# Queries and keys: split as token rows and turned by transposing transfers

## The chip, the cores and the metric

The program runs on one core of one Trainium2 chip. Its time is the device time in microseconds of one execution. Three executions of the kernel before took 1791.48, 1805.04 and 1810.17 us, median 1805.04. The core has five engines that run their own instruction streams in order: TensorE (PE, matrix products, with its weight loads as PEld), VectorE (DVE), ScalarE (ACT), GpSimd (POOL) and SyncE (SP), which here issues every transfer.

## The reference, cut to what matters

Sixteen images go through a template correlation (31x31 window, normalised by local mean and deviation), which gives 256 token rows of 256 features per image. Then, for each image:

```python
x = rmsnorm(h) * norm_w
q = (x @ Wq)  -> 16 heads of 64          k, v = x @ Wkv -> 8 heads of 64
q = q / |q| * (q_gamma + 1) * 8          k = k / |k| * (k_gamma + 1) * 8
sim = tanh(q @ k.T / 50) * 50 / 8        # 2 query heads share one key head
attn = softmax(causal(sim));  out = sum over heads(attn @ v) @ Wout
h = layernorm(h + out)
```

A five-matrix ternary network with gates and gelu and a second layer norm follow. The changed part is what lies between `x @ W` and `q @ k.T`: the length of each head's vector, the division by it, the gammas, the cut of each f32 value into a high and a low f16 part, and the turn from token rows (token on the partition) to feature rows (feature on the partition), which the product of queries and keys needs on both sides.

## The kernel before, in words

There are three stages: tokens (to 537 us of the profiled execution), attention (to about 1112 us) and the network (the rest). The change is in attention and in the last plane of the token stage, where the first image's attention inputs are made. Images go in groups of four, four groups; a group has 32 "heads" (8 per image, each a pair of query heads with one or two key heads).

Every engine runs the same list of named steps, each doing its own part, with semaphores between them. The list of a group comes from `attention_order` (L735): each step has a place on a scale on which head n's `score` stands at n, and the steps are sorted by it. The tables `IMAGE_AT`, `EDGE_AT` (first image of the next group) and `GROUP_AT` hold the places of the steps that make an image's inputs, counted from that image's first head. Since each engine keeps the order of its list, a step that waits holds up whatever stands behind it on its engine.

The steps, for one image and its two token blocks tb of 128 tokens:

- `make` (j = 4 tb + r): PE multiplies tokens by a 512-column piece of the weights (six matmuls); r = 0, 1 are queries, 2 keys, 3 values. ACT copies the result to `raw` (128 x 1536 f32 per block), or to `v` for r = 3.
- `square` and `sum`: ACT squares `raw` into `squares`, DVE sums each head's 64.
- `root`: DVE gets 1/length by three Newton rounds, eleven small instructions; one root per block.
- `scale`: DVE multiplies `raw` by it.
- `turn` (j = 4 tb + r, r = 0 to 2): PE transposes four 128x128 f32 pieces of `raw` into a bank of PSUM (`job`, four banks in a ring that all steps of the kind `make`, `turn`, `turn_h`, `turn_o`, `project` share). ACT writes the high f16 part, times gamma, to `q_hi` (four instructions of 128x128) or `k_hi` (one of 128x512).
- `low`: DVE subtracts that from the bank and writes `q_lo` or `k_lo`.
- `score` (n): PE, twelve short f16 matmuls into `sim`, which exists once; so head n's score waits for ACT's tanh of head n-1 (L1131). ACT then does tanh (L955) and exp (L958), POOL the causal mask (L888).
- `mix` (n), placed 2.5 places after its score: PE multiplies by `v`, DVE divides by the row sums (three short instructions, two for even heads).
- `turn_o`: PE transposes an image's output `o`, ACT copies it; `project`: PE multiplies by `Wout`, DVE adds it to h. The four `project` steps stand at the end of a group.

The `bits` steps read the network's weights piece by piece on DVE; SP loads each piece (`words`, L1198) and waits for the DVE step before.

Of the kernel before, what the change touches and what calls it, by code (L numbers as in the profile page):

```python
# [7 lines left out]
F16 = mybir.dt.float16  # L8
I32 = mybir.dt.int32
# [36 lines left out]
ROOTS = 1  # L46
# [5 lines left out]
BAND = RI * PR * TCOLS  # L52


class Shared:


    def __init__(self, nc, ctx):
# [31 lines left out]
        self.dump = sb("dump", [P, PR, D])  # L90
# [7 lines left out]
        self.o = sb("o", [P, 2, 2, HEADS, DH])  # L98
        sb("x_third_end", [P, plane - 4 * HEADS * DH])
# [12 lines left out]
        sb("xp_end", [P, XW - 4 * HEADS * (DH + 1)])  # L112
        self.job = ctx.enter_context(nc.psum_tensor("job", [P, BANKS, 512], F32))
# [50 lines left out]
def token_stage(nc, sh, at, X, XT, TF, TPAD, H, WORDS, WEIGHTS, WQKV, NW, GQ, GK):  # L164
# [6 lines left out]
    with ExitStack() as ctx:  # L171
# [11 lines left out]
        xt = sb("xt", [P, 2, XT_W])  # L183
# [48 lines left out]

        s_wlo_pool = sem("s_wlo_pool")
# [27 lines left out]
        def _(sp):  # L261
# [31 lines left out]
            def body(g, c, n, last):  # L293
# [53 lines left out]
        def _(act):  # L347
# [70 lines left out]
            def body(g, c, n, last):  # L418
# [14 lines left out]
                if more:  # L433
                    regroup(n + 1, 0)
                    regroup(n + 1, 1)
                    turned(n + 1, 0)
                else:
                    act.wait_ge(at.s_ones, 1)
                    at.scalar_steps(act, FIRST, 0, FIRST_PARTS["makes"])
                    act.wait_ge(sh.s_gamma, 10)  # L440
                    at.scalar_steps(act, FIRST, 0, FIRST_PARTS["turns"][0] + FIRST_PARTS["turns"][1])
# [10 lines left out]
        def _(dve):  # L452
# [6 lines left out]
            dve.sem_inc(at.s_ss, 1)  # L459

# [101 lines left out]
            def fold_span():  # L562
# [6 lines left out]
                dve.tensor_scalar(sh.gamma[:], sh.gamma[:], sh.span[:, 3:4], 1.0 / KEY_SCALE, ALU.mult, ALU.mult)\  # L569
                   .then_inc(sh.s_gamma, 1)  # L570
                dve.tensor_scalar(sh.span[:, 2:3], sh.span[:, 2:3], 1.0 / CLAMP, None, ALU.mult).then_inc(sh.s_gamma, 1)
                dve.wait_ge(sh.s_gamma, 10)

# [13 lines left out]
            def body(g, c, n, last):  # L587
# [21 lines left out]
                else:  # L609
                    at.vector_steps(dve, FIRST, 0, FIRST_PARTS["makes"])  # L610
                    scale(g, c, n, 0)
                    at.vector_steps(dve, FIRST, 0, FIRST_PARTS["turns"][0])
                    scale(g, c, n, 1)
                    at.vector_steps(dve, FIRST, 0, FIRST_PARTS["turns"][1])
# [6 lines left out]
        def _(pe):  # L621
# [19 lines left out]
            def correlate(c, n, b, start=0.0, end=1.0):  # L641
# [8 lines left out]
                size = len(terms)  # L650
                for t in range(int(start * size), int(end * size)):
                    x, i, xs, ws = terms[t]
# [6 lines left out]
                                    stop=(t == size - 1), skip_group_check=True)  # L659
                if end == 1.0:  # L660
                    ins.then_inc(s_conv, 1)
# [4 lines left out]
            def body(g, c, n, last):  # L666
                more = not (last and c == 2)
                if not more:
# [32 lines left out]
    ("make", 0): -8, ("make", 1): -8, ("make", 2): -7.725, ("square", 0): -7.18, ("make", 6): -6.997,  # L701
    ("sum", 0): -6.79, ("root", 0): -6.361, ("make", 4): -6.348, ("scale", 0): -6.321, ("make", 5): -5.839,
    ("make", 3): -5.512, ("square", 1): -5.39, ("sum", 1): -5.219, ("turn", 0): -4.545, ("make", 7): -4.423,
    ("root", 1): -4.413, ("low", 0): -4.389, ("turn", 1): -3.147, ("scale", 1): -2.767, ("low", 1): -2.619,
    ("turn", 2): -2.538, ("low", 2): -1.89, ("turn", 4): -1.49, ("low", 4): -1.23, ("turn", 5): -1.205,
    ("turn", 6): -1.068, ("low", 5): -1.063, ("low", 6): -0.99,
}
EDGE_AT = {
    ("make", 0): -8, ("make", 1): -8, ("make", 2): -8, ("square", 0): -7.718, ("make", 6): -6.743,
    ("sum", 0): -6.311, ("make", 4): -5.808, ("root", 0): -5.602, ("scale", 0): -5.343, ("make", 5): -4.841,  # L710
    ("square", 1): -4.533, ("make", 3): -3.75, ("sum", 1): -3.523, ("root", 1): -2.958, ("make", 7): -2.776,
    ("scale", 1): -1.653, ("turn", 0): -0.263, ("low", 0): 0.74, ("turn", 1): 1.01, ("turn", 2): 2.113,
    ("low", 1): 2.862, ("low", 2): 3.052, ("turn", 4): 3.86, ("low", 4): 4.18, ("turn", 5): 4.291,
    ("turn", 6): 4.697, ("low", 5): 4.751, ("low", 6): 4.828,
}
GROUP_AT = {
    ("rms_sum", 0): 4, ("rms_sum", 1): 6, ("rms_sum", 2): 8.635, ("rms_sum", 3): 15.072, ("turn_h", 0): 19.823,
    ("turn_h", 1): 19.97, ("turn_h", 2): 20.742, ("turn_h", 3): 21.416, ("project", 0): 36.821,
    ("project", 1): 37.209, ("project", 2): 37.906, ("project", 3): 38,
}  # L720
GROUP_AT.update({("rms_root", 0): 15.489, ("rms_scale", 0): 16.649, ("norm", 0): 38.109})
MIX_AT, TURN_O_AT, BITS_AT = LAG + 0.502, (1.332, 2.286), (2.334, 7.379)


def first_parts():

    tokens = [("turn_h", k) for k in range(4)]
    makes = [("make", 0, j) for j in (0, 1, 2)] + [("square", 0, 0), ("sum", 0, 0), ("root", 0, 0)]
    makes += [("make", 0, j) for j in (4, 5, 6)] + [("square", 0, 1), ("scale", 0, 0), ("sum", 0, 1), ("root", 0, 1)]
    makes += [("make", 0, j) for j in (3, 7)] + [("scale", 0, 1)]  # L730
    turns = [[(kind, 0, 4 * tb + r) for r in range(3) for kind in ("turn", "low")] for tb in range(2)]
    return {"tokens": tokens, "makes": makes, "turns": turns}
# [19 lines left out]
CHUNKS = 8  # L752
WORD_COLS = 2 * (D // P) * HID + 2 * (HID // P) * HID + (HID // P) * D
CW = WORD_COLS // (GROUPS * CHUNKS)


def emptied_on(step):

    if step[0] == "turn":
        return "queries" if step[2] % 4 < 2 else "keys"  # L760
# [3 lines left out]
class Stretch:  # L764


    def __init__(self, order, before, ahead):
        self.order, self.before, self.ahead = order, before, ahead
        self.jobs, self.counts = {}, []
        self.total = dict.fromkeys(("act", "dve", "queries", "keys"), 0)  # L770
        for step in order:
            job = ("turn",) + step[1:] if step[0] == "low" else step
            if step[0] in ("turn_h", "make", "turn", "turn_o", "project"):
                self.jobs[step] = len(self.jobs)
                self.counts.append(None)
                if step[0] == "turn":
                    continue
            elif step[0] != "low":
                continue
            on = emptied_on(job)  # L780
            self.total[on] += 1
            self.counts[self.jobs[job]] = (on, self.total[on])
# [10 lines left out]
FIRST = Stretch(FIRST_PARTS["tokens"] + FIRST_PARTS["makes"] + FIRST_PARTS["turns"][0] + FIRST_PARTS["turns"][1], False, 0)  # L793
# [11 lines left out]
class Attention:  # L805


    def __init__(self, nc, sh, ctx):
# [5 lines left out]
        self.rn, self.guess, self.slope = sh.rn, sh.guess, sh.slope  # L814
# [878 lines left out]
```

## Time and profile before

| | |
|---|---|
| median of three runs | 1805.04 us |
| profiled execution | 1788.73 us |
| its span on the core | 1786.9 us |
| mean granted TensorE clock | 0.994 of full speed |
| PE, DVE, ACT, POOL busy | 97, 64, 52, 24% |

The profiled execution is 0.9% under the median. A matmul's duration runs from its start to its modelled end, and the next one starts before that end; what a step costs on PE is therefore read from the distance between the starts of two steps, not from durations.

### The profile page before, as it was taken

The numbers are of one execution on the slowest core, as the hardware profiler recorded it, in microseconds if no ns is written. First come the engines' busy times: TensorE is split into PE (matmuls) and PEld (weight loads), VectorE is DVE, ScalarE is ACT, GpSimd is POOL, SyncE is SP. The second block draws the span as 40 slices with busy tenths as digits, with TensorE's granted clock in tenths as the row PEclk, the third lists the DMA queues.
The fourth block names the chain that finished last, engine by engine and source line by source line (L and its number), as shares of the span: only waits on it lengthen the run. The fifth ranks groups of instructions, "written<-read, shape, count | busy, mean of one in ns | idle before, by whom it ended". The sixth has DMA issues, their size and how long they took to land. (4 is left out here: it accounts for less than half of the span.)

```text
span 1786.9 us, 33009 instructions
## 1 busy us (share of the span) xinstructions
PE 1726.3 (97%) x12152; PEld 1509.7 (84%) x12152; DVE 1137.2 (64%) x2191; ACT 930.3 (52%) x1309; POOL 427.8 (24%) x515
## 2 busy tenths in 40 slices
PE   5999999999999999999999998999999999999998
PEld 5999998999987887888888887788888888888886
DVE  7899898898996877786877884423324141515242
ACT  8655555566658985895995994222222222222221
POOL 2000000000112222221222321434344333434343
PEclk9999999999999999999999999999999999999999
DMA  6322222223103002001100203600000000000000
GB/s 195 111 89 85 113 79 111 86 78 143 48 1 108 26 18 89 26 26 71 36 26 9 81 18 112 214 1 24 25 1 24 1 25 1 24 1 24 1 13 13
DMA packets 26421, 97.23 MB, mean 54 GB/s; under 512 B 3081, under 2 KB 11401, under 8 KB 21010
## 3 DMA queue, kind: packets, MB, share of 16 engines
q1 hardware_dynamic: 26258, 94.96, 15.5%
q8 instruction: 115, 1.88, 0.4%
q14 instruction: 48, 0.39, 0.1%
HBM read 82.33 MB, written 24.15 MB: 60 GB/s over the span
## 5 line engine op out<-in xcount | busy, mean ns | idle before, releaser
L658 PE MATMUL conv<-w,x 128*128 128x368 f16 (+5 forms) x3960 | 452.7, 277 | 3.8 <-issue 3.8
L658 PEld LDWEIGHTS conv<-w,x 128*128 128x128 f16 x3960 | 427.2, 146 | 27.9 <-issue 4.5
L1439 ACT ACTIVATE raw_c<-ring,sh 128x512 f32<-128x512 f32 x128 | 87.6, 689 | 334.3 <-PE ring L1542 334.2
L1451 DVE CAST ha_hi<-raw_c 128x512 fp32r<-128x512 f32 x128 | 85.2, 665 | 201.0 <-ACT raw_c L1439 198.8
L888 POOL TENSOR_SCALAR_AFFINE_SELECT probs<-probs 128x256 f32<-128x256 f32 x256 | 129.9, 530 | 342.2 <-ACT probs L958 342.2
L1398 POOL TENSOR_TENSOR ha_lo<-raw_c,ha_hi 128x512 fp32r<-128x512 f32 x128 | 165.3, 1291 | 189.5 <-DVE ha_hi L1451 189.5
L1542 PE MATMUL ring<-ha_hi,wh 128*128 128x512 f32 x512 | 199.4, 389 | 0.9 <-POOL ha_lo L1398 0.9
L1542 PE MATMUL ring<-ha_lo,wh 128*128 128x512 f32 x512 | 199.2, 389 | 0.0
L1542 PE MATMUL ring<-hb_lo,wh 128*128 128x512 f32 x512 | 199.2, 389 | 0.0
L1542 PE MATMUL ring<-hb_hi,wh 128*128 128x512 f32 x512 | 199.2, 389 | 0.0
L1151 PEld LDWEIGHTS mixed<-v,probs 128*128 128x128 f32 x1536 | 185.5, 193 | 10.7 <-POOL probs L888 1.7
L1151 PE MATMUL mixed<-v,probs 128*128 128x65 f32 x1536 | 192.2, 275 | 1.9 <-DVE o L1044 1.8
L1451 DVE CAST hb_hi<-raw_c 128x512 fp32r<-128x512 f32 x64 | 35.7, 558 | 187.3 <-ACT raw_c L1439 187.0
L379 ACT ACTIVATE lines<-job 128x512 f32<-128x512 f32 x96 | 50.0, 605 | 167.8 <-PE job L638 167.7
L955 ACT ACTIVATE probs<-sim,span 128x768 f32<-128x768 f32 x128 | 115.8, 905 | 12.6 <-PE sim L1136 12.0
L472 DVE TENSOR_TENSOR_SCAN box<-lines 128x271 f32<-128x271 f32 x192 | 120.2, 699 | 3.5 <-ACT lines L379 3.5
L1114 PE MATMUL job<-wqkv_hi,ht_hi 128*128 128x512 f32 x256 | 110.5, 432 | 7.6 <-PEq L171 3.6
L1398 POOL TENSOR_TENSOR hb_lo<-raw_c,hb_hi 128x512 fp32r<-128x512 f32 x64 | 82.5, 1290 | 140.5 <-DVE hb_hi L1451 140.5
L1542 PEld LDWEIGHTS ring<-ha_hi,wh 128*128 128x128 f32 x512 | 96.1, 188 | 21.6 <-POOL ha_lo L1398 1.6
L1542 PEld LDWEIGHTS ring<-hb_lo,wh 128*128 128x128 f32 x512 | 96.1, 188 | 20.0
L1542 PEld LDWEIGHTS ring<-ha_lo,wh 128*128 128x128 f32 x512 | 96.1, 188 | 19.9
L1542 PEld LDWEIGHTS ring<-hb_hi,wh 128*128 128x128 f32 x512 | 96.1, 188 | 19.9
(161 smaller groups left out, 3198.5 us busy)
## 6 DMA issues: line engine op xcount, KB each, us to landing
xt<-x_columns_in SPq DMA_DIRECT2D x12, 1163.0 KB, 5.2
xp<-x_patches_in SPq DMA_DIRECT2D x12, 1152.0 KB, 5.1
hidden_words<-hidden_weights_in SPq DMA_DIRECT2D x8, 1408.0 KB, 8.5
words<-hidden_words SPq DMA_DIRECT2D x32, 352.0 KB, 3.0
wh<-hidden_words SPq DMA_DIRECT2D x8, 1024.0 KB, 10.0
tokens<-planes SPq DMA_DIRECT2D x4, 1024.0 KB, 4.6
h<-tokens SPq DMA_DIRECT2D x4, 1024.0 KB, 7.3
attended<-h SPq DMA_DIRECT2D x8, 512.0 KB, 3.5
```

The costliest lines, as they stand in the source:

```text
L379: act.activation(dst, turn[:, k % 4], ACT.Copy).then_inc(s_across, 1)
L472: return dve.tensor_tensor_scan(out, line[:, TH:TH + SCAN], line[:, 0:SCAN], 0.0, ALU.add, ALU.subtract)
L658: ins = pe.matmul(out, xs[:, c, RI - 1 - i:RI - 1 - i + NR, :, x].rearrange("p r g -> p (r g)"), w, start=(t == 0), stop=(t == size - 1), ...
L888: ins = pool.affine_select(out=diag, in_=diag, compare_op=ALU.is_ge, fill=0.0, base=0, pattern=[[0, 2], [1, P]], channel_multiplier=-1)
L955: act.activation(self.probs[:, n % 4], self.sim[:, :, 0:3 * P], ACT.Tanh, scale=self.span[:, 2:3]).then_inc(self.s_tanh, 1)
L1114: ins = pe.matmul(bank, x[:, f, img % GI, P * tb:P * tb + P], w[:, f, 512 * r:512 * r + 512], start=(t == 0), stop=(t == len(terms) - 1))
L1151: ins = pe.matmul(out, self.probs[:, n % 4, m, at:at + P], self.v[:, img % 2, jb, 2 * (hd // 2) + m], start=(jb == 0), stop=(jb == ib), sk ...
L1398: pool.tensor_tensor(dst[1][:, u % KH], raw[:, u % 4], dst[0][:, u % KH].bitcast(F32), ALU.subtract).then_inc(s_lo, 1)
L1439: act.activation(raw[:, u % 4], bank, ACT.Gelu, scale=scale[:, m:m + 1]).then_inc(s_gelu, 1)
L1451: dve.tensor_copy(dst[0][:, u % KH], raw[:, u % 4]).then_inc(s_hi, 1)
L1542: ins = pe.matmul(bank, a, b, start=start, stop=False, skip_group_check=True)
```

## The change

High and low parts are now cut out of `raw` while the rows are still tokens, and four transfers that transpose on their way bring them to `q_hi`, `k_hi`, `q_lo`, `k_lo`. In detail:

- The gammas are held as rows (`gain`, 128 x 1024, two new inputs of 512 KB each, loaded at the end of the token stage); DVE folds them there. One `root` serves both token blocks of an image and ends with a small multiply by `KEY_SCALE`. `scale` gets a second DVE instruction, queries times `gain`.
- `turn` is gone. `high` is one ACT copy of 128 x 1536 to `hi_tok` (f16); `low` one DVE subtraction of 128 x 1536 to `lo_tok` (f16). Each buffer exists once: `high` waits until the transfers out of `hi_tok` have landed and until the `low` before it is done; `low` waits for `high` and for the transfers out of `lo_tok`.
- SP gets `sync_steps`: after each `high` and each `low` two transfers, 128 x 1024 (queries) and 128 x 512 (keys), f16, from SBUF to SBUF with transpose. The first head's `score` of an image waits for all eight transfers of the image.
- The tables have new places; first image, later images and the next group's first image now have the same ones. `turn_o` stands directly behind the `mix` of an image's last head. Some buffers move, and `dump` has two rows for eight.

```diff
 IMAGE_AT = {
-    ("make", 0): -8, ("make", 1): -8, ("make", 2): -7.725, ("square", 0): -7.18, ("make", 6): -6.997,
...
+    ("make", 0): -7.9, ("make", 1): -7.5, ("make", 2): -7.1, ("square", 0): -6.9, ("make", 4): -6.5,
+    ("make", 5): -6.0, ("sum", 0): -6.0, ("make", 6): -5.5, ("square", 1): -5.3, ("sum", 1): -4.8, ("root", 0): -4.2,
+    ("make", 3): -4.0, ("scale", 0): -3.8, ("make", 7): -3.5, ("high", 0): -3.2, ("low", 0): -2.9,
+    ("scale", 1): -2.6, ("high", 1): -2.0, ("low", 1): -1.7,
...
-MIX_AT, TURN_O_AT, BITS_AT = LAG + 0.502, (1.332, 2.286), (2.334, 7.379)
+MIX_AT, TURN_O_AT, BITS_AT = LAG + 0.5, (0.5, 0.51), (2.48, 6.48)
...
+    def sync_steps(self, sp, run, g, steps, between=None):
...
+                if kind == "high":
+                    sp.wait_ge(self.s_high, t + 1)
+                    sp.wait_ge(self.s_score, self.image(g, img) * HEADS + 8)
+                    settle(sp, self.s_settle)
+                    sp.dma_start(self.q_hi[:, img % 2, :, cols], self.hi_tok[:, 0:HEADS * P], transpose=True).then_inc(self.s_flip_hi, 16)
+                    sp.dma_start(self.k_hi[:, img % 2, :, cols], self.hi_tok[:, HEADS * P:QK], transpose=True).then_inc(self.s_flip_hi, 16)
...
-            elif kind == "turn":
...
-                        ins = act.activation(self.q_hi[:, img % 2, u, cols], bank[:, e * P:(e + 1) * P], ACT.Copy,
-                                             scale=self.gamma[:, u:u + 1])
...
+            elif kind == "high":
+                t = self.image(g, step[1]) * 2 + step[2]
+                act.wait_ge(self.s_qn, t + 1)
+                act.wait_ge(self.s_low, t + 2)
+                if run is not FIRST or step[2]:
+                    act.wait_ge(self.s_flip_hi, 32 * t)
+                act.activation(self.hi_tok[:], self.raw[:, step[2]], ACT.Copy).then_inc(self.s_high, 1)
...
-                dve.tensor_tensor(heads, heads, by, ALU.mult).then_inc(self.s_qn, 1)
+                dve.tensor_tensor(heads, heads, by, ALU.mult).then_inc(self.s_scaled, 1)
+                dve.wait_ge(self.s_scaled, t + 1)
+                queries = self.raw[:, tb, 0:HEADS * P]
+                dve.tensor_tensor(queries, queries, self.gain, ALU.mult).then_inc(self.s_qn, 1)
...
+                dve.wait_ge(self.s_high, t + 1)
+                if run is not FIRST or step[2]:
+                    dve.wait_ge(self.s_flip_lo, 32 * t)
+                dve.tensor_tensor(self.lo_tok[:], self.raw[:, step[2]], self.hi_tok[:], ALU.subtract).then_inc(self.s_low, 1)
...
-            elif kind == "turn":
-                img, tb, r = step[1], step[2] // 4, step[2] % 4
-                bank = free_bank(run, g, step)
-                pe.wait_ge(self.s_qn, self.image(g, img) * 2 + tb + 1)
-                for e in range(4):
-                    c = (4 * r + e) * P
-                    ins = pe.transpose(bank[:, e * P:(e + 1) * P], self.raw[:, tb, c:c + P], self.ident[:])
-                ins.then_inc(self.s_job, 1)
...
-                    pe.wait_ge(self.s_emptied["queries"], self.image(g, img) * 4 + 4)
-                    pe.wait_ge(self.s_emptied["keys"], self.image(g, img) * 2 + 2)
+                    pe.wait_ge(self.s_flip_hi, 64 * self.image(g, img) + 64)
+                    pe.wait_ge(self.s_flip_lo, 64 * self.image(g, img) + 64)
...
+                dve.wait_ge(s_rows, 32)
+                dve.tensor_scalar(sh.gain, sh.gain, 1.0, sh.span[:, 3:4], ALU.add, ALU.mult).then_inc(sh.s_gamma, 1)
...
-                    at.tensor_steps(pe, FIRST, 0, FIRST_PARTS["turns"][0])
-                    correlate(c, n, 3, 0.0, 0.5)
-                    at.tensor_steps(pe, FIRST, 0, FIRST_PARTS["turns"][1])
-                    correlate(c, n, 3, 0.5, 1.0)
+                    correlate(c, n, 3)
```

What the tables do is seen in ACT's list. In the changed kernel, for one image inside a group, from the tanh and exp of the fifth head before the image to those of the second before it (`v<-job` are the `make` steps of the values, `hi_tok<-raw` the two `high`):

```order
L980 ACTIVATE probs<-sim,span 128x768 [waits b_mix,b_score]
L983 ACTIVATE probs<-probs 128x768 [waits b_tanh]
...
L960 ACTIVATE v<-job 128x8x64 [waits b_mix,b_job]
L974 REGISTER_ALU [waits b_low,b_qn]
L975 ACTIVATE hi_tok<-raw 128x1536 [waits b_flip_hi]
...
L980 ACTIVATE probs<-sim,span 128x768 [waits b_mix,b_score]
L983 ACTIVATE probs<-probs 128x768 [waits b_tanh]
L972 REGISTER_ALU [waits b_qn]
L974 REGISTER_ALU [waits b_low]
L975 ACTIVATE hi_tok<-raw 128x1536 [waits b_flip_hi]
```

Two copies of 1536 columns, each with a wait for `b_qn` (the DVE `scale`), now stand between the tanh and exp of neighbouring heads. Before, the same engine had short pieces there, whose waits are for PE's `turn` (in brackets what an instruction waits for):

```order
L945 ACTIVATE q_hi<-job,gamma 128x128 [waits b_score,b_job]
L945 ACTIVATE q_hi<-job,gamma 128x128 x3
...
L955 ACTIVATE probs<-sim,span 128x768 [waits b_mix,b_score]
L958 ACTIVATE probs<-probs 128x768 [waits b_tanh]
L916 ACTIVATE ht_hi<-job 128x4x32x4 [waits b_job]
L949 ACTIVATE k_hi<-job 128x4x128 [waits b_score,b_job]
```

On DVE the changed list around the two `scale` steps of an image is (`raw<-raw,rn` and `raw<-raw,lines` are `scale`, `lo_tok` is `low`, `rl`, `o` and `parts` are `mix`):

```order
L1046 TENSOR_TENSOR raw<-raw,rn 128x1536
L1049 TENSOR_TENSOR raw<-raw,lines 128x1024
...
L1061 RECIPROCAL rl<-mixed 128x4
L1065 TENSOR_TENSOR o<-mixed,rl 128x2x128
...
L1055 TENSOR_TENSOR lo_tok<-raw,hi_tok 128x1536
L1046 TENSOR_TENSOR raw<-raw,rn 128x1536
L1049 TENSOR_TENSOR raw<-raw,lines 128x1024
```

The first `low` stands between the two `scale` steps and waits for ACT's first `high`; before, both roots and both scales had `turn` pieces between them.

## Rows read from the trace of the kernel before

**Rows 1.** The page, busy time of each engine over the span:
```profile
PE 1726.3 (97%) x12152; PEld 1509.7 (84%) x12152; DVE 1137.2 (64%) x2191; ACT 930.3 (52%) x1309; POOL 427.8 (24%) x515
```

**Rows 2.** Waits of PE, 560 to 1060 us: total, times, longest:
```profile
PE mixed L1151 <- DVE o L1044: 1.8, 2, 1.4
```

**Rows 3.** Busy time by windows, attention: start:end, length, busy (count), clock, DMA, GB/s:
```profile
1000.00:1060.00 60.00, 60.00 (x517) 51.16 (x517) 46.44 (x123) 53.45 (x87) 15.53 (x30) 1.00 0.09 26
```

**Rows 4.** Timeline of PE, attention: start, duration, instruction:
```profile
696.14 1.45 PE L1151 MATMUL mixed<-v,probs 128*128 128x65 f32 x12
697.52 0.28 PE L1136 MATMUL sim<-q_hi,k_hi 64*128 64x256 f16 x2
...
698.12 0.66 PE L1123 MATMUL job<-ident,raw 128*128 128x128 f32 x4
698.62 1.45 PE L1151 MATMUL mixed<-v,probs 128*128 128x65 f32 x12
699.88 0.48 PE L1114 MATMUL job<-wqkv_hi,ht_hi 128*128 128x512 f32 x1
...
701.45 0.28 PE L1136 MATMUL sim<-q_hi,k_hi 64*128 64x256 f16 x2
```

**Rows 5.** Groups by line and shape, 560 to 1060 us: count, busy, mean ns, idle before:
```profile
L955 ACT ACTIVATE probs<-sim,span 128x768 f32<-128x768 f32 x112 | 101.4, 905 | 10.0 <-PE sim L1136 9.5
L958 ACT ACTIVATE probs<-probs 128x768 f32<-128x768 f32 x111 | 93.8, 845 | 3.5
L1018 DVE TENSOR_TENSOR raw<-raw,rn 128x1536 f32<-128x1536 f32 x28 | 49.8, 1778 | 0.4
L990 DVE TENSOR_REDUCE rn<-lines 128x24 f32<-128x1536 f32 x28 | 49.0, 1749 | 7.7 <-ACT lines L936 7.5
L924 ACT ACTIVATE raw<-job 128x512 f32<-128x512 f32 x84 | 49.0, 587 | 66.8 <-PE job L1114 66.7
L936 ACT ACTIVATE lines<-raw 128x1536 f32<-128x1536 f32 x28 | 41.5, 1480 | 0.7
L1048 DVE TENSOR_TENSOR o<-o,parts 128x256 f32<-128x256 f32 x56 | 24.8, 443 | 1.9
L1044 DVE TENSOR_TENSOR parts<-mixed,rl 128x256 f32<-128x256 f32 x56 | 23.8, 424 | 1.9
```

**Rows 6.** Timeline of DVE, one root, first and last of eleven instructions:
```profile
646.19 0.38 DVE L996 TENSOR_SCALAR rn<-rn 128x24 f32<-128x24 f32 x1
...
648.56 0.18 DVE L1011 SCALAR_TENSOR_TENSOR rn<-slope_b,guess_b 128x24 f32<-128x24 f32 x1
```

**Rows 7.** DMA issues of the page and the view: KB each, us to landing:
```profile
w<-padded_template SPq DMA_DIRECT2D x6, 636.0 KB, 9.3
out<-y SPq DMA_DIRECT2D x16, 256.0 KB, 2.5
xt<-w_qkv_in SPq DMA_DIRECT2D x1, 1024.0 KB, 7.0
```

**Rows 8.** Timeline of PE, the `project` steps that end a group:
```profile
1099.64 10.31 PE L1172 MATMUL job<-w_out,ot 128*128 128x256 f32 x47
```

**Rows 9.** Timeline of PE around its longest wait in attention:
```profile
708.51 2.79 PE L1151 MATMUL mixed<-v,probs 128*128 128x65 f32 x12 [1.35 <-DVE o L1044]
711.10 2.76 PE L1123 MATMUL job<-ident,raw 128*128 128x128 f32 x12
```

**Rows 10.** Busy time by windows of 5 us, columns as in rows 3:
```profile
710.00:715.00 5.00, 5.00 (x32) 4.29 (x31) 4.75 (x18) 2.94 (x11) 0.77 (x2) 0.50 0.02 3
1090.00:1095.00 5.00, 2.91 (x23) 2.43 (x22) 3.01 (x8) 1.14 (x2) 0.30 (x1) 1.00 0.00 0
```

**Rows 11.** Timeline of DVE and PE, last plane of the token stage:
```profile
481.71 5.01 DVE L472 TENSOR_TENSOR_SCAN box<-lines 128x271 f32<-128x271 f32 x8
...
490.22 0.15 DVE L564 TENSOR_SCALAR span<-span 128x1 f32<-128x1 f32 x1
...
522.44 1.49 PE L1123 MATMUL job<-ident,raw 128*128 128x128 f32 x12
```

More of the change, by code:

```diff
@@ L45 @@
 QK = QH * DH + HEADS * DH
-ROOTS = 1
+ROOTS = 2
 BANKS = 4
@@ L300, in body @@
                     sp.dma_start(WORDS[rows], WEIGHTS[rows]).then_inc(s_copies, 16)
+                if last and c == 2:
+                    sp.wait_ge(s_box, 2 * LAST + 4)
+                    for dst, src in ((sh.gain, GQ_ROWS), (sh.gain_k, GK_ROWS)):
+                        sp.dma_start(dst, src).then_inc(s_rows, 16)
+                    at.sync_steps(sp, FIRST, 0, FIRST_PARTS["flips"])
                 if c == 2:
@@ L649, in correlate @@
                 quarter = 4 * PC * b
-                size = len(terms)
-                for t in range(int(start * size), int(end * size)):
-                    x, i, xs, ws = terms[t]
+                for t, (x, i, xs, ws) in enumerate(terms):
                     first = PC * (x - 1)
@@ L700 @@
 IMAGE_AT = {
-    ("make", 0): -8, ("make", 1): -8, ("make", 2): -7.725, ("square", 0): -7.18, ("make", 6): -6.997,
[L702 to L705, printed above, removed]
@@ L710 @@
[L710 to L714, printed above, removed]
+    ("make", 0): -7.9, ("make", 1): -7.5, ("make", 2): -7.1, ("square", 0): -6.9, ("make", 4): -6.5,
@@ L715 @@
+    ("make", 5): -6.0, ("sum", 0): -6.0, ("make", 6): -5.5, ("square", 1): -5.3, ("sum", 1): -4.8, ("root", 0): -4.2,
+    ("make", 3): -4.0, ("scale", 0): -3.8, ("make", 7): -3.5, ("high", 0): -3.2, ("low", 0): -2.9,
+    ("scale", 1): -2.6, ("high", 1): -2.0, ("low", 1): -1.7,
 }
 GROUP_AT = {
-    ("rms_sum", 0): 4, ("rms_sum", 1): 6, ("rms_sum", 2): 8.635, ("rms_sum", 3): 15.072, ("turn_h", 0): 19.823,
-    ("turn_h", 1): 19.97, ("turn_h", 2): 20.742, ("turn_h", 3): 21.416, ("project", 0): 36.821,
@@ L725, in first_parts @@
+GROUP_AT.update({("rms_root", 0): 18.4, ("rms_scale", 0): 20.4, ("norm", 0): 39})
+MIX_AT, TURN_O_AT, BITS_AT = LAG + 0.5, (0.5, 0.51), (2.48, 6.48)
 def first_parts():
     tokens = [("turn_h", k) for k in range(4)]
-    makes = [("make", 0, j) for j in (0, 1, 2)] + [("square", 0, 0), ("sum", 0, 0), ("root", 0, 0)]
-    makes += [("make", 0, j) for j in (4, 5, 6)] + [("square", 0, 1), ("scale", 0, 0), ("sum", 0, 1), ("root", 0, 1)]
-    makes += [("make", 0, j) for j in (3, 7)] + [("scale", 0, 1)]
@@ L731, in first_parts @@
-    turns = [[(kind, 0, 4 * tb + r) for r in range(3) for kind in ("turn", "low")] for tb in range(2)]
-    return {"tokens": tokens, "makes": makes, "turns": turns}
+    makes = [("make", 0, j) for j in (0, 1, 2)] + [("square", 0, 0), ("sum", 0, 0)]
+    makes += [("make", 0, j) for j in (4, 5, 6)] + [("square", 0, 1), ("sum", 0, 1), ("root", 0, 0)]
+    makes += [("make", 0, j) for j in (3, 7)]
+    flips = [("scale", 0, 0), ("high", 0, 0), ("scale", 0, 1), ("low", 0, 0), ("high", 0, 1), ("low", 0, 1)]
```

191 lines of the change are left out of this document (102 added, 89 removed).

## The prediction

> **What bounds the kernel now.** I read the page first: PE is busy 97% of the span, every other engine far less [rows 1]. So a step taken off PE is worth its full length wherever PE never waits. Whether it waits in attention is told by the waits of PE from 560 to 1060 us: six kinds, 8.7 us in all of 500, the longest single one 1.35 us for DVE's `mix` [rows 2, 9]. The windows then say how near the others are: in a full stretch of 60 us ACT is busy 53.5 and DVE 46.4 [rows 3]. PE is the bound, ACT is six us behind it, and the present order lets ACT and DVE work in short pieces under PE's cover.
>
> The costs on PE come from distances between starts [rows 4]: `mix` 1.4 us (696.14 to 697.52), `score` 0.6 (697.52 to 698.12), four transposes of a `turn` 0.50 (698.12 to 698.62), one `make` 1.45 to 1.57 (699.88 to 701.45). The four `project` steps of a group are 32 matmuls with two records each; at 10.31 us for 47 records [rows 8] the 64 are 14 us.
>
> **Removed from PE.** 90 `turn` steps in the attention stage (six for each of 15 images) at 0.50 us: 45 us; the first image's six are two lots of 12 transposes of about 1.3 us in the token stage [rows 11]: 2.7 us. Together **-47.7 us**, all of it on the path as long as PE stays the bound.
>
> **Moved and added on ACT and DVE.** Both engines get less work: ACT loses the q_hi and k_hi pieces and gets two copies of 1536 columns; DVE loses one of two roots. Busy time is not what matters, though: the new order makes one long chain between two points of PE's own list. I walk it for one image inside a group. M is the moment when PE ends `make` 6, the last that fills `raw`; all times are us after M. Durations are the means of [rows 5] unless said.
>
> - ACT ends an exp, copies the bank (0.59) and squares (1.48): 2.7. DVE sums (1.75): 4.4; a `mix` (0.44 + 0.42 + about 0.18 for the small one): 5.5; the root, eleven instructions in 2.55 us [rows 6]: 8.1. `scale` is 1.78, and the multiply by `gain` by the same rate 1024/1536 of that, 1.19: 11.1.
> - ACT, which keeps its order, has waited for that with `high`. A copy of 1536 columns is nearest to the square of the same size, 1.48: 12.6. Only now comes the tanh (0.9) of the head behind it: 13.5.
> - PE has between M and there four `mix`, three `score` less one, two `make`: 4 x 1.4 + 2 x 0.6 + 2 x 1.45, and the score whose tanh is late, 0.6: 10.3. The next `score` needs the tanh at 13.5, since `sim` exists once. **PE waits 3.2 us.**
> - DVE does a `mix`, then `low` for block 0 (1.78, as the f32 `scale` of that size) from 12.6 to 14.4, then `scale` and `gain` of block 1 (3.0): 17.4. ACT's second `high` ends at 18.9, the next tanh at 19.8. PE, done with a `score` and a `mix` at 15.5, **waits 4.3 us**; it then has a `score` and a `mix`, until 21.8.
> - DVE's `low` of block 1 ends at 20.7. Then two transfers (393 KB) must land before the image's first `score`. With L for that pair, PE **waits L - 1.1 us**.
>
> **The price of the transfers, L.** No transposing transfer is in the trace. Queries' 262 KB are like the 256 KB of the output, which land in 2.5 us [rows 7]; that is the low bound. The transfer with the smallest pieces is w<-padded_template, 636 KB in 9.3 us [rows 7]; at its rate the pair takes 5.7 us. A transpose handles small pieces, so I go nearer to the second: L = 4.5. If the pair does not only take that long to land but occupies the path for it, four pairs of an image line up behind each other from 12.6 on: at 5.7 each the last lands at 12.6 + 22.8 = 35.4, and the last wait is 13.6 instead of 3.4. Another such price sits beside these: by the Trainium skill, "Advanced Engine Details and Errata", section "X-Bar Transpose (TRN2)", a transposing transfer runs about as fast as a plain one; the sum would then lie at the low bound of L, some 24 us under mine.
>
> **Counted.** Twelve images (the second to fourth of each group, and in the last group too) have all three waits: 12 x (3.2 + 4.3 + 3.4) = **+131 us**. The first images of groups 2 to 4 are made at the end of the group before; there the `project` steps, 14 us, lie between the last `low` and the first `score` and cover the transfers: 3 x 7.5 = **+22 us**. `turn_o` now stands directly behind the `mix` that it needs; DVE takes 1.04 us and the way there and back for it, while before a score and a make lay between: 1.3 us x 12 = **+16 us**. The waits of before are contained in the new ones: **-9 us**.
>
> **Token stage.** fold_span ran at 490.2 us [rows 11]. It now waits for 2 x 512 KB that are asked for when the box sums are done, 486.7 [rows 11]; one MB took 7.0 us to land [rows 7], so 3.5 us of waiting, and two multiplies of 1024 columns, 2.4. The weights' low parts, for which PE's first `make` waits, stand behind these on DVE and come later by that: **+6 us**. SP's queue costs nothing more: `words` loads have 5 to 10 us between request and use, and the stores at the end of a group come before the next group's first `high`.
>
> **Clock.** After the 1.35 us wait at 707 us PE's granted clock was 0.50 in the next window, the 1.2 GHz level, and `mix` took 2.6 us for 1.4 [rows 9, 10]; in the window 1090 to 1095, with PE idle 2.1 us, it stayed at 1.00 [rows 10]. So a wait may cost some 3 us more, or nothing. Slow work between two waits is hidden in them; behind the third wait it is not. I take 2.4 us for twelve: **+29 us** (both ends: 0, and 3.2 us also after each `turn_o`, 77).
>
> **Sum.** -47.7 + 131 + 22 + 16 - 9 + 6 + 29 = +147 on the profiled 1788.7: 1936. The median of the runs before lies 16 us above that execution; with nearly all of this added, the forecast is **1950 us**, 8% slower.
>
> **Rivals.**
>
> 1. *The chain has slack and only PE's saving is left.* For it speaks that ACT and DVE get less work and that the durations of `low` and `gain` are mine. It needs the chain of 20.7 us to be shorter by ten, since PE's own work beside it is 14 us. Then 1789 - 48 - 9 + 6: about 1740. Chance 8%. Half of that slack ends near the old time, within 1%: 4%.
> 2. *The transfers themselves are the bound.* If a pair occupies the path for twice the slow row's price, 11.4 us, the four pairs of an image end at 12.6 + 45.6 = 58.2, the last wait is 36 us instead of 3.4, and twelve of them make +390; the three covered images add about 50: 2380 us. It decides from about 8 us a pair, where they pass my range. Against it is that this is half the rate of the slowest large transfer in the rows, and no more than that. A rule of the Trainium skill would do this: "VectorE: DVE Perf Modes", section "The three transpose paths", gives 1309 ns for a 128x128 block by transfer, against 390 ns on TensorE. By it, an estimate, a pair of 12 blocks would take 15.7 us and the time would be about 2650. This trace puts the TensorE side at 0.125 us a block [rows 4], well under that page's figure, so I do not lean on its other one. Chance 12%.
> 3. *My forecast*, between 1835 and 2120: chance 76%.
>
> **Range.** Low end: L = 2.5 (-24), no clock loss (-29), half of the two ACT waits (-56): 1950 - 109, 1840. High end: pairs that line up at 5.7 us (+122) and the clock's upper bound (+48): 2120. With the small tails inside, 1835 to 2120 holds about 8 in 10. About 1% is what a measurement of this kernel can tell from none (its runs spread over 1%): faster 0.08, same 0.04, slower 0.88.
>
> **What would show it.** In the profile of the changed kernel: PE's waits in attention grow from 9 us per 500 to over 100, and name ACT's tanh (L980) and the transfers, for `sim`; ACT sits idle before `hi_tok` for DVE's `raw`, about 3 us each; `turn_o` waits for `o`; the landing of q_lo and k_lo gives L directly; the clock is under 0.99 in attention. Wrong would be: a chain that keeps ahead of PE, so that PE is still busy without waits; or landings above 8 us, which make SP's queue the chain.

## The result, and the profile after

The changed kernel takes 2000.48 us (median of four executions, 1992.07 to 2004.81) against 1805.07 us: a ratio of 1.1106, 95% interval 1.1047 to 1.1166. It is 11% slower; forecast were 1950 us and 8%. The profiled execution took 2004.05 us, its span is 2002.2 us, 215 us above that of before.

The page of the changed kernel; the second row is TensorE's granted clock in tenths, in 40 slices of the span. Its first row answers to [rows 1]:

```profile
PE 1801.3 (90%) x11768; PEld 1563.9 (78%) x11768; DVE 1129.5 (56%) x1809; ACT 897.4 (45%) x1053; POOL 444.7 (22%) x515
PEclk9999999999977868877788777579999999999999
DMA packets 129073, 122.99 MB, mean 61 GB/s; under 512 B 105513, under 2 KB 113833, under 8 KB 123698
```

PE has 384 fewer instructions and is busy 75 us *longer*. The clock row says where: only in the attention stage. The same stage by windows (start:end, length, busy of PE, PEld, DVE, ACT, POOL, clock, DMA share, GB/s), from the store of the tokens to the end of the last `project`, first before, then after:

```profile
537.00:1110.00 573.00, 558.11 (x4584) 475.69 (x4584) 426.16 (x1145) 451.77 (x768) 142.68 (x272) 0.99 0.15 49
```
```profile
538.00:1328.00 790.00, 634.56 (x4224) 531.49 (x4224) 415.29 (x785) 421.40 (x528) 159.00 (x272) 0.78 0.27 65
```

The stage has all of the change: 573 became 790, +217. ACT and DVE are busy less than before, as read from the diff. PE's idle time (length less busy) went from 15 to 155 us, **+140**; its busy time from 558 to 635, **+77**, though 45 us of transposes are gone from it. So, by subtraction, some 77 + 45 = **122 us** are time that matmuls took longer than before, at a mean clock of 0.78 for 0.99.

What PE waits for over the whole span (total, times, longest), where [rows 2] had DVE's `mix` alone on top:

```profile
PE sim L1149 <- ACT probs L980: 95.6, 30, 4.4
PE job L1173 <- DVE o L1069: 19.5, 16, 1.3
PE job L666 <- ACT down_m L391: 19.0, 2, 16.5
PE sim L1149 <- DMA k_lo<-lo_tok: 15.2, 8, 2.5
PE sim L1149 <- issue: 12.1, 5, 3.4
```

The third row is in the kernel before as well, outside attention. The first is the tanh behind a `high`, twice for each of 15 images. Three of the five `issue` waits, 1.9 us each, stand where an image's wait for `k_lo` stands, in the last group; so the third waits are 21.0 us in eleven images. The other two, 3.35 and 3.05 us, stand right behind `project`, when the transfers had long landed; what they are for isn't shown. ACT's own waits from 545 to 1320 us say why the tanh is late:

```profile
ACT hi_tok L975 <- DVE raw L1049: 109.2, 30, 4.5
```

**One image walked.** PE, DVE and ACT around the second image, each row with start, duration and in brackets the idle time before it and its releaser. `make` 6 ends at 597.18, which is M of the prediction.

```profile
597.18 1.45 PE L1164 MATMUL mixed<-v,probs 128*128 128x65 f32 x12
...
606.17 1.55 PE L1164 MATMUL mixed<-v,probs 128*128 128x65 f32 x12
611.03 0.40 PE L1149 MATMUL sim<-q_hi,k_hi 64*128 64x256 f16 x2 [3.31 <-ACT probs L980]
612.10 2.82 PE L1164 MATMUL mixed<-v,probs 128*128 128x65 f32 x12
617.59 0.39 PE L1149 MATMUL sim<-q_hi,k_hi 64*128 64x256 f16 x2 [2.67 <-ACT probs L980]
618.66 2.82 PE L1164 MATMUL mixed<-v,probs 128*128 128x65 f32 x12
624.01 0.40 PE L1149 MATMUL sim<-q_hi,k_hi 64*128 64x256 f16 x2 [2.53 <-DMA k_lo<-lo_tok]
```
```profile
607.36 1.22 DVE L1049 TENSOR_TENSOR raw<-raw,lines 128x1024 f32<-128x1024 f32 x1
610.31 1.76 DVE L1055 TENSOR_TENSOR lo_tok<-raw,hi_tok 128x1536 f16<-128x1536 f32 x1 [1.17 <-ACT hi_tok L975]
...
616.98 1.76 DVE L1055 TENSOR_TENSOR lo_tok<-raw,hi_tok 128x1536 f16<-128x1536 f32 x1 [0.89 <-DMA k_lo<-lo_tok]
```
```profile
608.70 1.48 ACT L975 ACTIVATE hi_tok<-raw 128x1536 f16<-128x1536 f32 x1 [3.64 <-DVE raw L1049]
610.09 0.88 ACT L980 ACTIVATE probs<-sim,span 128x768 f32<-128x768 f32 x1
```

`gain` ends at M + 11.4 (forecast 11.1), `high` at 13.0 (12.6), the late tanh at 13.8 (13.5), and PE waits 3.31 us (3.2). This is the chain that the prediction walked. PE stands 3.3 us, ACT has stood 3.6 before it, and DVE works without a pause up to the end of `gain`. What follows differs: the `mix` at 612.10 takes 2.82 us, twice its 1.45, so PE arrives at the second wait later and finds 2.67 us of it left (forecast 4.3).

The windows of the same 40 us show the clock itself, with columns as above:

```profile
600.00:605.00 5.00, 5.00 (x39) 4.05 (x39) 4.49 (x15) 3.92 (x6) 1.02 (x3) 1.00 0.02 5
605.00:610.00 5.00, 2.72 (x30) 2.38 (x29) 4.00 (x6) 1.36 (x2) 0.51 (x2) 0.89 0.00 0
610.00:615.00 5.00, 3.90 (x24) 3.33 (x24) 4.66 (x3) 1.81 (x3) 2.99 (x2) 0.50 0.56 107
615.00:620.00 5.00, 2.41 (x18) 2.02 (x19) 4.01 (x8) 4.70 (x8) 1.77 (x3) 0.50 0.67 127
620.00:625.00 5.00, 2.47 (x19) 2.00 (x19) 1.33 (x4) 2.55 (x9) 0.78 (x3) 0.50 0.81 155
625.00:630.00 5.00, 5.00 (x18) 3.91 (x14) 0.00 (x0) 2.34 (x3) 0.76 (x2) 0.56 0.01 4
630.00:635.00 5.00, 5.00 (x39) 4.05 (x38) 0.61 (x2) 3.48 (x8) 0.00 (x0) 1.00 0.00 0
```

Full (2.4 GHz) until the first wait, half (1.2 GHz) through all three waits, and full again only some 6 us after the last, while PE is in the `make` that follows: some 20 us at half speed for this image, of which PE works some 13. The last image of the last group has no `make` behind its first score, only `mix`, `score` and `turn_o`. There the clock stays at half from its first score, 1268 us, until PE is in `project`, 1314 us: 42 us of work, some 21 of them for the clock (an estimate, half of the work, from the two levels). One window out of it:

```profile
1282.00:1287.00 5.00, 5.00 (x33) 4.27 (x35) 0.87 (x4) 1.74 (x2) 1.53 (x4) 0.50 1.02 416
```

**The transfers.** SP's issues of the second block of that image, and the view's rows for all 128 (median us from issue to landing at the end), in the place of [rows 7]:

```profile
616.85 1.23 SPq L887 DMA_TRANSPOSE q_hi<-hi_tok  x1
618.12 1.28 SPq L888 DMA_TRANSPOSE k_hi<-hi_tok  x1
619.59 1.23 SPq L893 DMA_TRANSPOSE q_lo<-lo_tok  x1
620.87 1.29 SPq L894 DMA_TRANSPOSE k_lo<-lo_tok  x1
```
```profile
q_hi<-hi_tok SPq DMA_TRANSPOSE x32, 3.2
k_hi<-hi_tok SPq DMA_TRANSPOSE x32, 2.5
q_lo<-lo_tok SPq DMA_TRANSPOSE x32, 3.2
k_lo<-lo_tok SPq DMA_TRANSPOSE x32, 2.6
```

262 KB land in 3.2 us. But the issue instructions hold SP for 1.25 us each, one after the other. The last `low` ended at 618.74; SP, still issuing for `high`, began on q_lo at 619.59, and PE went on at 624.01: 5.3 us for the pair, of which 3.4 are SP's.

### The profile page after: what moved, and what is told of

It reads as the page before. It is cut to its first block and busy times, and to the rows that moved or that the text cites. A ratio compares the mean times of both kernels' runs of the same rounds, so it can differ in the third digit from the quotient of the medians.

```text
span 2002.2 us, 31467 instructions
## 1 busy us (share of the span) xinstructions
PE 1801.3 (90%) x11768; PEld 1563.9 (78%) x11768; DVE 1129.5 (56%) x1809; ACT 897.4 (45%) x1053; POOL 444.7 (22%) x515
## 2 busy tenths in 40 slices
DMA packets 129073, 122.99 MB, mean 61 GB/s; under 512 B 105513, under 2 KB 113833, under 8 KB 123698
## 5 line engine op out<-in xcount | busy, mean ns | idle before, releaser
L914 POOL TENSOR_SCALAR_AFFINE_SELECT probs<-probs 128x256 f32<-128x256 f32 x256 | 146.8, 597 | 518.9 <-ACT probs L983 518.9
L1164 PEld LDWEIGHTS mixed<-v,probs 128*128 128x128 f32 x1536 | 238.9, 239 | 14.4 <-issue 6.3
L1164 PE MATMUL mixed<-v,probs 128*128 128x65 f32 x1536 | 246.4, 324 | 0.0
L1474 DVE CAST ha_hi<-raw_c 128x512 fp32r<-128x512 f32 x128 | 90.6, 708 | 201.0 <-ACT raw_c L1462 198.8
L1149 PE MATMUL sim<-q_hi,k_hi 64*128 64x256 f16 (+1 forms) x512 | 73.9, 284 | 127.0 <-ACT probs L980 95.6
L1061 DVE RECIPROCAL rl<-mixed 128x4 f32<-128x4 f32 x128 | 22.7, 177 | 229.5 <-PE mixed L1164 229.5
L1149 PEld LDWEIGHTS sim<-q_hi,k_hi 64*128 64x128 f16 x512 | 27.9, 104 | 158.6 <-ACT probs L980 100.4
L1135 PE MATMUL job<-wqkv_hi,ht_hi 128*128 128x512 f32 x256 | 121.0, 473 | 10.1 <-DVE ht_lo L1010 9.8
```

The lines of the kernel that those rows point to most:

```text
L914: ins = pool.affine_select(out=diag, in_=diag, compare_op=ALU.is_ge, fill=0.0, base=0, pattern=[[0, 2], [1, P]], channel_multiplier=-1)
L1135: ins = pe.matmul(bank, x[:, f, img % GI, P * tb:P * tb + P], w[:, f, 512 * r:512 * r + 512], start=(t == 0), stop=(t == len(terms) - 1))
L1149: ins = pe.matmul(self.sim[:, m, 2 * P * jb:2 * P * jb + P * (2 - jb)], k[rows, img % 2, hd // 2, P * jb:P * jb + P], q[rows, img % 2, hd, ...
L1164: ins = pe.matmul(out, self.probs[:, n % 4, m, at:at + P], self.v[:, img % 2, jb, 2 * (hd // 2) + m], start=(jb == 0), stop=(jb == ib), sk ...
L1474: dve.tensor_copy(dst[0][:, u % KH], raw[:, u % 4]).then_inc(s_hi, 1)
```

## The experiments

All are of one core. Each is compared with runs of the kernel before on the same chip; the ratio is to them. Differences in us to the changed kernel (2000.48) are across chips, on which the medians of the kernel before lie up to 6 us apart; small ones mean little. For each stage the windows run between the same two points as above.

**Only the tables.** The changed kernel, its steps placed anew so that every link of an image's chain has work of PE beside it. Steps move by up to 3.6 places (entries set several to a line here); the tables of the next group's first image and of the group's own steps are fitted anew likewise and not shown:

```diff
 IMAGE_AT = {
-    ("make", 0): -7.9, ("make", 1): -7.5, ("make", 2): -7.1, ("square", 0): -6.9, ("make", 4): -6.5,
-    ("make", 5): -6.0, ("sum", 0): -6.0, ("make", 6): -5.5, ("square", 1): -5.3, ("sum", 1): -4.8, ("root", 0): -4.2,
-    ("make", 3): -4.0, ("scale", 0): -3.8, ("make", 7): -3.5, ("high", 0): -3.2, ("low", 0): -2.9,
-    ("scale", 1): -2.6, ("high", 1): -2.0, ("low", 1): -1.7,
+    ("make", 1): -11.13, ("make", 0): -9.99, ("make", 2): -9.85, ("square", 0): -9.16, ("sum", 0): -8.17,
+    ("make", 4): -8.15, ("make", 6): -7.87, ("make", 5): -7.67, ("square", 1): -7.38, ("sum", 1): -7.3,
+    ("root", 0): -6.33, ("scale", 0): -5.77, ("make", 3): -5.03, ("make", 7): -4.98, ("high", 0): -4.69,
+    ("low", 0): -4.45, ("scale", 1): -3.98, ("high", 1): -2.48, ("low", 1): -2.18,
...
-MIX_AT, TURN_O_AT, BITS_AT = LAG + 0.5, (0.5, 0.51), (2.48, 6.48)
+MIX_AT, TURN_O_AT, BITS_AT = LAG + 0.5, (1.79, 2.71), (0.31, 7.01)
```

> The changed kernel with other numbers in IMAGE_AT, EDGE_AT, GROUP_AT and TURN_O_AT and nothing else: every instruction is the same, only their order in each engine's list differs. The makes of an image begin some two to four places earlier, high and low stand where DVE and ACT have already finished what they wait for, turn_o 1 stands two places later. If the loss is the ACT-DVE chain against PE's list (my reading), the 127 us of waits for sim fall under 40 and most of the clock loss goes with them: 1760 to 1830 us. If the transfers or the work they need are the bound, the order is of no use: 1950 us or more.

Measured 1826.72 us, ratio 1.0128 (1.0062 to 1.0195): 174 us less than the changed kernel, by the order alone. From `make` 6 to `high` 0 there are now 3.2 places instead of 2.3, and from `scale` 1 to `high` 1 1.5 instead of 0.6. The waits of PE over the span, and the stage:

```profile
PE sim L1190 <- ACT probs L1021: 12.3, 9, 2.4
```
```profile
538.00:1148.00 610.00, 557.32 (x4224) 467.48 (x4224) 411.08 (x785) 418.93 (x528) 159.79 (x272) 0.91 0.36 84
```

95.6 us of waits for the tanh have become 12.3, and with them the clock rose from 0.78 to 0.91. The change itself is not what costs 11%; its tables are. Yet the median is still 16 us above that of before, and the profiled stage 37 us longer than before, not 45 shorter. One place shows part of why: before the last image's first score PE stands until 1089.60 (SP issued `k_lo` at 1086.08), and the rows after it are at half speed for 45 us (first window, last of them, and the one after):

```profile
1089.60 0.40 PE L1190 MATMUL sim<-q_hi,k_hi 64*128 64x256 f16 x2 [4.57 <-issue]
```
```profile
1090.00:1095.00 5.00, 5.00 (x38) 4.27 (x33) 1.50 (x3) 2.13 (x3) 0.76 (x2) 0.50 0.50 139
...
1130.00:1135.00 5.00, 3.78 (x10) 2.84 (x9) 0.00 (x0) 1.46 (x2) 0.13 (x1) 0.50 0.00 0
1135.00:1140.00 5.00, 5.00 (x23) 4.30 (x23) 1.44 (x3) 0.00 (x0) 0.00 (x0) 0.94 0.00 0
```

**The clock apart from the waits.** PE does idle transposes, which nothing reads, where it would stand: 24 and 32 ahead of the two late scores, 12 ahead of an image's first, 8 ahead of `turn_o`.

```diff
+                fill = {0: 12, 6: 24, 7: 32}.get(hd, 0) if n and (run is BODY or n < 25) else 0
+                if fill:
+                    ahead = next(s for s in run.order[run.order.index(step):] if s in run.jobs)
+                    spare = free_bank(run, g, ahead)
+                    for _ in range(fill):
+                        pe.transpose(spare[:, 0:P], self.ident[:], self.ident[:])
...
                 bank = free_bank(run, g, step)
+                for _ in range(0 if b else 8):
+                    pe.transpose(bank[:, 0:P], self.ident[:], self.ident[:])
```

> The changed kernel, with idle work on PE just before its predicted waits: 24, 32 and 12 transposes of the identity (0.11 us each at full clock, into a free bank of job) before the score of the seventh and eighth head of an image and of the first of the next, and 8 before the first turn_o. Nothing reads them. If the lower granted clock is what makes the loss larger than the waits alone, the granted clock in attention rises from 0.79 to over 0.92 and the time falls by 50 to 90 us, to 1910 to 1950. If the clock matters little, because slow work hides in the waits, the time stays at 2000 or grows.

Measured 1967.67 us, ratio 1.0896 (1.0830 to 1.0962), 33 us less than the changed kernel, less than expected. The stage:

```profile
538.00:1291.00 753.00, 673.43 (x5336) 582.06 (x5336) 415.19 (x785) 420.33 (x528) 163.74 (x272) 0.95 0.30 68
```

The clock did come back, 0.78 to 0.95; the waits for the tanh fell to 31.2 us. But the 1112 added transposes are themselves PE work, 0.125 us each by [rows 4], 139 us, and not all of it lies where PE would have stood. So this run shows that the clock comes back when PE's standing is filled, and that it leaves the stage 37 us shorter, the fill's own time paid; it isn't a clean measure of what the slow clock costs. **With about half of that fill**:

```diff
-                fill = {0: 12, 6: 24, 7: 32}.get(hd, 0) if n and (run is BODY or n < 25) else 0
+                fill = {0: 6, 6: 16, 7: 16}.get(hd, 0) if n and (run is BODY or n < 25) else 0
...
-                for _ in range(0 if b else 8):
+                for _ in range(0 if b else 5):
```

> As e2_warm, with 16, 16 and 6 idle transposes before the three scores and 5 before turn_o, where e2 had 24, 32, 12 and 8: 43 in all instead of 76 for each image, 3.6 us less of added work, 54 us over fifteen images. If e2 gained only 33 us because its added work was longer than the waits, less of it is better as long as the clock holds: 1935 to 1960. If the clock falls again with the shorter filling: 1970 to 2000.

Measured 1970.93 us, ratio 1.0929 (1.0851 to 1.1006): no gain over the full fill. The stage's clock is 0.89, the waits for the tanh 56.5 us. Less fill gave lower clock and longer waits in like measure. The second of the two expectations held.

**Is it the transposing?** The four kinds of transfer move the same bytes to the same tiles without transposing; the queries and keys are then not the right ones.

```diff
-                    sp.dma_start(self.q_hi[:, img % 2, :, cols], self.hi_tok[:, 0:HEADS * P], transpose=True).then_inc(self.s_flip_hi, 16)
+                    sp.dma_start(self.q_hi[:, img % 2, :, cols], self.hi_tok[:, 0:HEADS * P].rearrange("p (e t) -> p e t", t=P)).then_inc(self.s_flip_hi, 16)
```

> The changed kernel with its 128 transposing transfers made plain copies of the same bytes between the same buffers, so q_hi to k_lo hold token rows (attention is computed on untransposed data). By the chain theory the transfers only set the last of the three waits (15 us of waits for k_lo in all): 1980 to 2002 us. If transposing is what costs, through its landing, SP's issue time of 1.25 us each, or what it does to other engines: under 1930.

Measured 1997.80 us, ratio 1.1061 (1.0995 to 1.1127), 2.7 us under the changed kernel, within the latter's spread (1992.07 to 2004.81). The landings, and PE's waits:

```profile
q_hi<-hi_tok SPq DMA_DIRECT2D x32, 256.0 KB, 2.9
k_lo<-lo_tok SPq DMA_DIRECT2D x32, 128.0 KB, 3.0
```
```profile
PE sim L1149 <- ACT probs L980: 95.5, 30, 4.6
PE sim L1149 <- DMA k_lo<-lo_tok: 7.3, 6, 1.3
```

The waits for `k_lo` halve; SP issues a plain transfer in 0.6 to 0.7 us. The two ACT waits stay. So transposing is not the cost. A plain copy is a transfer too, so that transfers as such are no bound (rival 2) is shown by their landings and by the retimed kernel, which has the same 128 of them.

**Is it the chain?** The multiply by `gain`, 1.26 us, is left out of each `scale`; queries lack their gamma.

```diff
-                dve.tensor_tensor(heads, heads, by, ALU.mult).then_inc(self.s_scaled, 1)
-                dve.wait_ge(self.s_scaled, t + 1)
-                queries = self.raw[:, tb, 0:HEADS * P]
-                dve.tensor_tensor(queries, queries, self.gain, ALU.mult).then_inc(self.s_qn, 1)
+                dve.tensor_tensor(heads, heads, by, ALU.mult).then_inc(self.s_qn, 1)
```

> The changed kernel without the second instruction of scale (queries times gain, 128 x 1024 on DVE); the queries' gammas are left out. Chain theory: each image has two of them, 1.15 us each, on the path between make 6 and the last low, for 15 images 35 us, and a little clock: 1945 to 1975. If DVE is not on the path: 1995 to 2005.

Measured 1962.16 us, ratio 1.0852 (1.0785 to 1.0919): 38 us less (by the ratios, 46), for 32 x 1.26 = 40 us of DVE work, on an engine that is busy half of the stage. Waits for the tanh are 76.2 instead of 95.6; the stage is 41 us shorter, half of it idle time, half PE's busy time at a clock of 0.80 instead of 0.78. DVE is on the path, between PE's `make` 6 and ACT's `high`, as walked.

**`turn_o` in both directions.** In the kernel before it is put directly behind its `mix`; in the changed one it is put back to the places of before.

```diff
-MIX_AT, TURN_O_AT, BITS_AT = LAG + 0.502, (1.332, 2.286), (2.334, 7.379)
+MIX_AT, TURN_O_AT, BITS_AT = LAG + 0.502, (0.51, 0.52), (2.334, 7.379)
```
```diff
-MIX_AT, TURN_O_AT, BITS_AT = LAG + 0.5, (0.5, 0.51), (2.48, 6.48)
+MIX_AT, TURN_O_AT, BITS_AT = LAG + 0.5, (1.332, 2.286), (2.48, 6.48)
```

> The kernel before with one number pair of the change: turn_o directly behind the mix of an image's last head (TURN_O_AT 0.51, 0.52 for 1.332, 2.286). As predicted, PE waits 1.3 us for o at each of the sixteen: +10 to +25 us, more where the clock falls after it. If the wait is hidden otherwise: within 5 us of the kernel before.

Measured 1820.87 us, ratio 1.0128 (1.0066 to 1.0189), about 15 us against the 1806.21 of before; PE waits for `o` 23.1 us in 16, where before it was 4.5 in 5.

> The changed kernel with turn_o at the places of before (1.332, 2.286). If the 19.5 us of waits for o are lost time of their own, 1970 to 1990; if they only delay PE where it waits for ACT or DVE anyway, within 5 us of 2000.

Measured 1983.59 us, ratio 1.1009 (1.0953 to 1.1066), 17 us less than the changed kernel, and PE waits for `o` only 5.1 us. The term of +16 stands, from both sides: these waits are lost time of their own.

**What is PE's saving worth?** The kernel before, with one transpose of the four in each `turn`; three quarters of queries and keys aren't turned. PE loses 96 x 3 x 0.125 = 36 us of work (32 at the 0.11 us that the expectation takes).

```diff
-                for e in range(4):
+                for e in range(1):
```

> The kernel before with one of the four transposes of each turn step (the other three pieces of queries and keys are left out), to measure what the PE work that the change removes is worth by itself. By the forecast's price of 0.11 us each, 288 transposes are 32 us: 1770 to 1780 if PE is the bound throughout. If ACT or DVE, whose work stays, takes over: 1790 to 1806.

Measured 1805.02 us, ratio 1.0010 (0.9969 to 1.0050) in ten executions against thirteen: nothing. The stage:

```profile
537.00:1127.00 590.00, 565.89 (x4314) 473.93 (x4314) 424.09 (x1145) 447.51 (x768) 139.32 (x269) 0.93 0.14 47
```

In the stage PE has 270 transposes less, 34 us, yet it is busy 566 us, 8 more than in the profile of before, and idle 24 instead of 15. The granted clock is 0.93 for 0.99. The two profiles are not alike, though: that of before is one of its shorter executions. Among executions of 1807 to 1809 us those of before have a mean clock of 0.980 to 0.983 over the whole span, these 0.969 to 0.972. One hundredth of the clock is some 18 us of PE's work (an estimate, 1734 x 0.0105), so about half of the 36 us came back as slower work; the rest should be waits, but no profile of such an execution of before was taken. The time fell in the range expected if ACT or DVE takes over, which is only a part of it.

The longest stretch at half clock starts at the first score of the last image. PE, now earlier there, waits 2.40 us for DVE's `k_lo` (first row), where before it waited 1.19 (second). After it the clock is 0.50 until `project`, 45 us later; in the kernel before it stays at 1.00 through the same steps (a window of each):

```profile
1069.50 0.28 PE L1136 MATMUL sim<-q_hi,k_hi 64*128 64x256 f16 x2 [2.40 <-DVE k_lo L1032]
1070.57 0.28 PE L1136 MATMUL sim<-q_hi,k_hi 64*128 64x256 f16 x2 [1.19 <-DVE k_lo L1032]
```
```profile
1080.00:1100.00 20.00, 20.00 (x127) 17.53 (x126) 4.69 (x13) 9.76 (x12) 3.45 (x10) 0.50 0.49 179
1075.00:1095.00 20.00, 17.18 (x184) 15.48 (x178) 10.88 (x27) 13.44 (x17) 6.55 (x14) 1.00 0.50 184
```

That stretch holds 40 us of work, some 20 of them for the clock (estimated as above). The runs do not show what decides whether a wait is followed by half clock: in the kernel before, one of 1.35 us was [rows 9, 10].

**Both together.** The retimed kernel, with idle transposes at the places where it still stands:

```diff
+                warm(run, g, step, {2: 18, 24: 34 if run is FINAL else 6}.get(n, 0))
...
+                warm(run, g, step, 9 if (img, b) == (3, 0) else 0)
...
+                    warm(run, g, step, 9)
```

(`warm` is the loop of the fill above; another 16 stand ahead of a group's first `make` of the next.)

> e1_retimed with idle transposes of the identity at the waits that its profile still shows on PE: 18 before the score of a group's third head, 34 before the first score of the last image of the last group (6 in the others), 9 before that image's turn_o and before project, 16 before the next group's first make. If the 16 us that e1 lies above the kernel before are the clock (it was at 0.50 from 1090 to 1135 us), it is near 1.00 there and the time is 1775 to 1805, at or under the kernel before. If they are work or waits, it stays at 1820 to 1835.

Measured 1801.41 us in twelve executions, ratio 0.9990 (0.9960 to 1.0020): on a level with the kernel before, not better. The stage:

```profile
538.00:1129.00 591.00, 561.25 (x4468) 477.17 (x4468) 411.94 (x785) 417.97 (x528) 163.53 (x272) 0.96 0.37 87
```

244 added transposes, some 30 us of work by the same price, bring the clock from 0.91 to 0.96 and the stage from 610 to 591. In the last image, after 34 of them, the clock is back at full long before `project`:

```profile
1090.00:1095.00 5.00, 5.00 (x64) 4.38 (x62) 1.22 (x4) 3.54 (x5) 0.96 (x3) 1.00 0.88 307
```

No version beats the kernel before by what can be measured.

## Why the prediction was right, and where its sizes were off

- **Mechanism and direction: right.** The walk's times held within 0.4 us up to the first wait; leaving out `gain` and moving the steps alone confirm that the chain DVE, ACT, PE of one image against PE's own order is what costs. Rival 1 (slack) is refuted by the 30 waits, rival 2 by the landing of 3.2 us, where it needed 8 for a pair, and by the retimed kernel.
- **The waits: near, in part by luck.** Terms for new waits gave 131 + 22 + 16 - 9 = 160; PE's idle time grew by 140. The waits for the tanh are 95.6 where 15 x 7.5 = 112 were forecast; the second is shorter than walked because the slow `mix` ahead of it fills part of it, which the prediction said of slow work between waits but did not subtract. Waits that it lacked make up for some of this: 6.4 us in two scores behind `project`, which it took as covered; 6.8 us in three of an image's `make` for `ht_lo`; 4.7 us in four of `project` for `ot` (1.6 in one before). `turn_o` waits at all sixteen images, 19.5 us, not at twelve.
- **L: too small, and for another reason.** Walked with 4.5, measured 5.3 us at the second image. Its size isn't the landing (3.2 and 2.6) but SP, which each issue holds for 1.25 us. Still the third wait came out at 2.53 us there and 21.0 us in eleven images, not 12 x 3.4 = 41: at the second image PE reached it 2.5 us later than walked, again at half clock. By the Trainium skill, "Advanced Engine Details and Errata", section "X-Bar Transpose (TRN2)", transposing transfers run about as fast as plain ones; the landings agree (3.2 against 2.9 us for 262 KB). The Trainium skill, "VectorE: DVE Perf Modes", section "The three transpose paths", gives 1309 ns for a 128x128 block by transfer. As a price per block of a larger transfer, which is how the estimate of 15.7 us for a pair took it, this does not hold here: eight such blocks land in 3.2 us, not 10.5.
- **The clock: the term that failed.** It was +29 (2.4 us for each of twelve images, bounds 0 and 77). Some 122 us of longer work were found in the stage, above the upper bound; part of it lies between waits and shortens them. The bound came from one 1.35 us wait [rows 9, 10] and took the price of a single wait. What the trace shows after the change is three waits in 20 us, and the clock at half from the first until some 6 us behind the last, and half clock for all of the last image, some 21 us more.
- **-47.7 for the transposes: mis-sized.** They are gone, but 36 us of the same kind taken off the kernel before gave 0 (interval -0.3 to +0.5%). The premise, that a step off PE is worth its full length where PE never waits, fails there. This is not a second loss beside the clock's; much of it is the same, work saved and given back at a lower clock. In sum the stage has +140 for waits instead of 160, and -45 + 122 = +77 for work instead of -48 + 29 = -19; these make +217 against +141. Of the 76 us between, the token stage (+1 for +6) and the network stage (674 us for 677) take back 8; the median after lies 4 us under its profile, and the forecast stood 14 us above its own sum. That leaves the 50 us by which the result lies above the forecast.
- **The range held, and not by its clock term.** With the clock at its upper bound and all else as summed it would have ended at 1998 us, under the result. It was as wide as 2120 because of pairs of transfers that line up (+122), which no run shows: the landings stay at 3.2 us.
- **Token stage: +6 forecast, +1.2 measured.** The tokens' store is issued at 537.48 instead of 536.33 us. The rows of the gammas landed in 3.6 and 4.4 us instead of the 7.0 taken.

## What to carry to other kernels

Where the order of work is a table fitted to the steps, merging steps invalidates it: short pieces fitted between neighbours' work, 128 x 1536 pieces with a wait in front do not fit there. Walk one unit of work along the engines before building, and judge a design only after its table has been fitted to it (here 2000 became 1827 us). And on an engine that is busy 97%, don't count removed work as time; measure that by leaving the work out, before building what replaces it.

## What the runs showed of the hardware that was not expected

- A transposing transfer from SBUF to SBUF holds the issuing SP some 1.25 us (128 x 1024 and 128 x 512 alike), a plain one of the same bytes 0.6 to 0.7 us, most from DRAM some 0.35. The packets rose from 26421 to 129073, 105513 of them under 512 B. The plain copies make nearly as many, 127025, so that is not the transposing; and the retimed kernel with idle transposes has 129074 of them and takes as long as the kernel before.
- In the retimed kernel one wait of 4.57 us was followed by 45 us at 1.2 GHz, in which PE stood still for only 2.5 us; in the kernel with one transpose a wait of 2.40 us by some 45 us, and the changed kernel's last image ran at half clock from 1268 to 1314 us. In all three PE did only `mix`, `score` and `turn_o`, and the clock rose in `project`. At the second image it was back 6 us behind the last wait, with PE in `make`. In the kernel before, the same last image ran at full clock. What decides whether and when the clock falls or rises stays open.
- With 6% less work for PE in the stage, in the same order, the kernel took as long. Its mean clock over the span was about 0.01 lower than in executions of before of equal length.
